# Decoder block on one core: transposed scores in the scores' four PSUM banks, a ring of four banks, and the projection moved ahead of the transposed scores

## What is computed

```python
x = layernorm(x + self_attention(x))        # causal; q and k normed per head, gains, biases
x = layernorm(x + cross_attention(x, ctx))  # rotary q and k, biases
x = layernorm(x + experts(x))               # 8 experts, top 2, 256 -> 512 -> 256, gelu
# attention: dot = q k^T ; att = softmax(dot) ; out = (att v) Wo + bo
```

## Time and profile before

| | us |
|---|---|
| median of 3 runs (lowest, highest) | 1186.8 (1186.4, 1188.1) |
| the profiled execution | 1184.3 |
| its span, first to last instruction | 1182.6 |
| busy in the span: PE / DVE / ACT / POOL | 1033.5 / 720.5 / 597.2 / 268.0 |
| mean granted clock of TensorE, share of full speed | 0.952 |

### The profile page before, as it was taken

One profiled execution on the slowest core, in us unless ns is written; L12 is line 12 of the kernel. 1 busy time (PEld: TensorE's weight loads), 2 busy tenths in 40 slices (PEclk: granted clock), 3 DMA queues, 4 the chain that ended last, 5 costly groups with the idle time before them and its releaser, 6 DMA issues.

```text
span 1182.6 us, 29067 instructions
## 1 busy us (share of the span) xinstructions
PE 1033.5 (87%) x10925; PEld 769.5 (65%) x10925; DVE 720.5 (61%) x1584; ACT 597.2 (51%) x1024; POOL 268.0 (23%) x309
## 2 busy tenths in 40 slices
PE   6899999999999999998999999876379999999930
PEld 3556666666666666666666666544269999999930
DVE  4656666666677777676768777763524444444446
ACT  3567767767755666565555555644122222222225
POOL 1053332322233200001212111132512222222210
PEclk9999999999999999999999999998579999999975
DMA  7117446455440001000000100011167766777656
GB/s 286 29 41 252 136 162 199 133 180 182 132 134 20 20 12 46 11 11 30 30 30 30 36 23 30 12 40 39 68 199 216 215 215 215 216 216 213 204 198 250
DMA packets 95078, 139.25 MB, mean 118 GB/s; under 512 B 11264, under 2 KB 68992, under 8 KB 93920
## 3 DMA queue, kind: packets, MB, share of 16 engines
q1 hardware_dynamic: 88320, 114.98, 31.2%
q0 software_dynamic: 6624, 22.42, 4.9%
HBM read 76.56 MB, written 60.29 MB: 116 GB/s over the span
## 4 chain that ended last, share of the span: by engine, by line
PE 80%; issue 6%; DVE 6%; ACT 4%; DMA 3%; SPq 1%; another core or an unknown queue 0%; ACTq 0%; DVEq 0%; POOLq 0%
PE PS L824 11%; PE PS L561 11%; PE PS L835 10%; PE PS L582 10%; PE PS L531 5%; PE PS L639 5%; PE PS L635 5%; PE PS L706 4%; PE PS L653 4%; PE PS L680 3%; PE PS L538 2%; PE PS L669 2%; ACT pT L904 2%; PE PS L534 2%; DVE part L1158 1%
## 5 line engine op out<-in xcount | busy, mean ns | idle before, releaser
L1158 DVE TENSOR_REDUCE part<-PS 128x6 f32<-128x768 f32 (+1 forms) x256 | 269.9, 1087 | 126.9 <-PE PS L538 84.8
L904 ACT ACTIVATE pT<-PS 128x768 f32<-128x768 f32 (+1 forms) x256 | 220.9, 915 | 94.1 <-PE PS L561 92.1
L561 PE MATMUL PS<-big 32*128 32x256 f32 (+1 forms) x2048 | 133.5, 373 | 21.3 <-issue 13.7
L1595 POOL TENSOR_SCALAR_AFFINE_SELECT pT<-pT 128x512 f32<-128x512 f32 x128 | 84.5, 661 | 279.0 <-ACT pT L904 275.4
L824 PEld LDWEIGHTS PS<-oT,big 128*128 128x128 f32 x1136 | 139.5, 194 | 5.4 <-ACT oT L1034 1.8
L824 PE MATMUL PS<-oT,big 128*128 128x128 f32 x1136 | 140.2, 277 | 1.0 <-ACT oT L1034 1.0
L561 PEld LDWEIGHTS PS<-big 32*128 32x128 f32 x2048 | 96.2, 185 | 64.3 <-issue 62.9
L582 PE MATMUL PS<-pT,vaug 128*32 128x256 f32 (+1 forms) x2048 | 126.3, 364 | 10.4 <-DVE carry L1365 2.3
L835 PE MATMUL PS<-w2s,qkn 128*128 x568 | 134.5, 380 | 0.2 <-issue 0.2
L1034 ACT ACTIVATE oT<-PS 128x256 f32<-128x256 f32 x71 | 27.3, 384 | 191.9 <-PE PS L813 191.9
L915 ACT ACTIVATE oT<-PS 128x256 f32<-128x256 f32 x128 | 49.1, 384 | 143.9 <-PE PS L582 125.0
(11 more groups left out here) (170 smaller groups left out, 1535.9 us busy)
## 6 DMA issues: line engine op xcount, KB each, us to landing
big<-w SPq DMA_DIRECT2D x71, 512.0 KB
xs_dram<-zrow SPq DMA_DIRECT2D x24, 1496.0 KB, 9.2
oT<-xs_dram SPq DMA_DIRECT2D x71, 136.0 KB
xin<-xT SPq DMA_DIRECT2D x16, 256.0 KB, 2.9
w2s<-w POOLq DMA_DIRECT2D x1, 4096.0 KB, 16.4
xb<-x SPq DMA_DIRECT2D x16, 256.0 KB, 11.2
xin<-ctxT SPq DMA_DIRECT2D x16, 256.0 KB, 2.8
big<-nmaxT SPq DMA_DIRECT2D x128, 4.0 KB
```

The source lines that it names most:

```text
L561: ins = pe.matmul(o, keys, a[r0:r1, 0, g, q0:T], start=True, stop=True)
L904: act.activation(pT[:, k % 2, 2 * half:2 * half + 2, 0:wide], src, ACT.Exp).then_inc((exp_a, exp_b)[half], 1)
L1158: dve.tensor_reduce(dst, src, AX.X, ALU.max, negate=True).then_inc((max_a, max_b)[half], 1)
L1595: pool.affine_select(d, d, [[0, 2], [0, 2], [1, P]], ALU.is_ge, 0.0, base=0, channel_multiplier=-1).then_inc(masked, 1)
```

## The change

It gives the transposed scores the same four banks as the scores, and the ring the other four (4 to 7). The score now waits for `exp_b` too, and `score_T` for `max_b` too. On PE `weigh` is followed by the quarter's projection, and `score_T` comes behind it, ahead of the quarter's last turn; for q >= 136, when no scores are left, `score_T` still comes first. `rate` moves ahead of `project_qk` 1, with its place in the ring. ACT's order follows (drains of the projections ahead of `weights`, `exp_gap` at the end); DVE takes the logits in quarter r = 1 instead of r = 2 and both maxima in one go for r = 2; POOL's scatter waits for the next quarter's scores; two start-up results change banks, and one of them is drained a quarter earlier.

```diff
@@ -37,6 +37,8 @@
 NORM_GROUPS = (4, 4, 8, 8, 4, 4)
+
+RING_BANKS = 4
 CHUNKS = 11
@@ -103,10 +105,10 @@
         elif r == 1:
+            n = block_at(q, LOGITS_AT)
+            place("logits", n, n is not None and crossed(n))
             place("qk1", block_at(q, QK_AT + 1))
             place("qT", block_at(q, TURN_Q))
-            n = block_at(q, LOGITS_AT)
-            place("logits", n, n is not None and crossed(n))
         elif r == 2:
@@ -265,8 +267,8 @@
-        S_BANK, ST_BANK = (2, 3, 0, 1), (2, 3, 4, 5)
-        S_HALF, ST_HALF = (PS[:, 1024:2048], PS[:, 0:1024]), (PS[:, 1024:2048], PS[:, 2048:3072])
+        S_BANK = ST_BANK = (2, 3, 0, 1)
+        S_HALF = ST_HALF = (PS[:, 1024:2048], PS[:, 0:1024])
@@ -278,8 +280,7 @@
         xin_in, xb_in = sems("xin_in", 2), sems("xb_in", 2)
-        ring_filled = [sem("ring_filled_0"), sem("ring_filled_1")]
-        ring_drained = [sem("ring_drained_0"), sem("ring_drained_1")]
+        ring_filled, ring_drained = sems("ring_filled", RING_BANKS), sems("ring_drained", RING_BANKS)
         squared, head_var = sem("squared"), sem("head_var")
@@ -329,26 +330,26 @@
         def ring_slot(job):
-            return bank(6 + RING[job] % 2)
+            return bank(RING_BANKS + RING[job] % RING_BANKS)
         def filled_by(job):
-            return ring_filled[RING[job] % 2]
+            return ring_filled[RING[job] % RING_BANKS]
         def drained_by(job):
-            return ring_drained[RING[job] % 2]
+            return ring_drained[RING[job] % RING_BANKS]
...
-            if RING[job] >= 2:
-                pe.wait_ge(drained_by(job), RING[job] // 2)
+            if RING[job] >= RING_BANKS:
+                pe.wait_ge(drained_by(job), RING[job] // RING_BANKS)
...
-            eng.wait_ge(filled_by(job), RING[job] // 2 + 1)
+            eng.wait_ge(filled_by(job), RING[job] // RING_BANKS + 1)
...
-            eng.wait_ge(drained_by(job), RING[job] // 2 + 1)
+            eng.wait_ge(drained_by(job), RING[job] // RING_BANKS + 1)
@@ -509,11 +510,13 @@
                     pe.wait_ge(exp_a, before + 1)
+                    pe.wait_ge(exp_b, before + 1)
                 a = qkT[:, n % 3]
...
                         pe.wait_ge(mask_ready, 1)
+                        pe.wait_ge(bo_ready, 1)
                     for j in range(STRIPS):
@@ -548,6 +551,7 @@
                     pe.wait_ge(max_a, NG * other[0] + other[1] + 1)
+                    pe.wait_ge(max_b, NG * other[0] + other[1] + 1)
                 if k >= 1:
@@ -751,14 +755,14 @@
                 for c in range(KC):
-                    ins = pe.matmul(bank(4)[:, 0:E], bvT[:, c, :], wx_o[:, c, :], start=(c == 0),
+                    ins = pe.matmul(bank(0)[:, 0:E], bvT[:, c, :], wx_o[:, c, :], start=(c == 0),
                                     stop=(c == KC - 1))
...
             for j in range(STRIPS):
-                ins = pe.transpose(bank(5)[:, j * P:(j + 1) * P], columns4[:, j, :], ident[:])
+                ins = pe.transpose(bank(3)[:, j * P:(j + 1) * P], columns4[:, j, :], ident[:])
             ins.then_inc(mask_pe, 1)
@@ -771,24 +775,27 @@
                     score_T(group_at(q, EXP_AT), q)
-                    weigh(group_at(q, WEIGH_AT))
-                else:
-                    weigh(group_at(q, WEIGH_AT))
-                    score_T(group_at(q, EXP_AT), q)
+                weigh(group_at(q, WEIGH_AT))
                 if r == 0:
                     project_qk(block_at(q, QK_AT), 0)
-                    turn_x2(block_at(q, LN_AT))
                 elif r == 1:
+                    rate(block_at(q, LOGITS_AT))
                     project_qk(block_at(q, QK_AT + 1), 1)
-                    turn_qk("qT", block_at(q, TURN_Q), 0)
-                    rate(block_at(q, LOGITS_AT))
                 elif r == 2:
...
                     project_v(block_at(q, V_AT))
-                    turn_qk("kT", block_at(q, TURN_K), 1)
                 else:
...
                     project_o(block_at(q, PROJECT_AT))
+                if q < NG * BLOCKS + SCORE_AT:
+                    score_T(group_at(q, EXP_AT), q)
+                if r == 0:
+                    turn_x2(block_at(q, LN_AT))
+                elif r == 1:
+                    turn_qk("qT", block_at(q, TURN_Q), 0)
+                elif r == 2:
+                    turn_qk("kT", block_at(q, TURN_K), 1)
+                else:
                     count_tokens(routed_at(q, RANK_AT))
@@ -1008,22 +1015,26 @@
                     seed_roots(block_at(q, CHAIN_AT), block_at(q, ROOT_AT))
-                    exp_gap(routed_at(q, RANK_AT))
                     drain_onT(block_at(q, PROJECT_AT))
                 drain_pv(group_at(q, WEIGH_AT))
+                if r == 0:
+                    drain_qk(block_at(q, QK_AT), 0)
+                elif r == 1:
+                    drain_qk(block_at(q, QK_AT + 1), 1)
+                elif r == 2:
+                    drain_v(block_at(q, V_AT))
+                else:
+                    drain_x1T(block_at(q, TURN_X1))
                 weights(group_at(q, EXP_AT), 0)
...
                 if r == 0:
-                    drain_qk(block_at(q, QK_AT), 0)
                     drain_x2T(block_at(q, LN_AT))
                 elif r == 1:
-                    drain_qk(block_at(q, QK_AT + 1), 1)
                     drain_turned("qT", block_at(q, TURN_Q), 0)
                 elif r == 2:
-                    drain_v(block_at(q, V_AT))
                     drain_turned("kT", block_at(q, TURN_K), 1)
                 else:
-                    drain_x1T(block_at(q, TURN_X1))
+                    exp_gap(routed_at(q, RANK_AT))
@@ -1088,7 +1099,7 @@
             dve.wait_ge(mask_pe, 1)
-            dve.tensor_copy(strips[:].rearrange("p j q -> p (j q)"), bank(5)).then_inc(mask_ready, 1)
+            dve.tensor_copy(strips[:].rearrange("p j q -> p (j q)"), bank(3)).then_inc(mask_ready, 1)
             dve.memset(ohb[:], 0.0)
@@ -1135,7 +1146,7 @@
                 dve.wait_ge(vbias_pe, 1)
-                dve.tensor_tensor(bo[:, 1], bank(4)[:, 0:E], bo[:, 1], ALU.add).then_inc(bo_ready, 1)
+                dve.tensor_tensor(bo[:, 1], bank(0)[:, 0:E], bo[:, 1], ALU.add).then_inc(bo_ready, 1)
@@ -1394,12 +1405,12 @@
                     choose_second(routed_at(q, SECOND_AT))
+                    take_logits(block_at(q, LOGITS_AT))
                     rotate(block_at(q, QK_AT + 1), 1)
                 elif r == 2:
-                    take_logits(block_at(q, LOGITS_AT + 1))
                     maxima(group_at(q, SCORE_AT), 0)
+                    maxima(group_at(q, SCORE_AT), 1)
                     divide(block_at(q, OUT_AT), 0)
-                    maxima(group_at(q, SCORE_AT), 1)
                     divide(block_at(q, OUT_AT), 1)
@@ -1418,7 +1429,7 @@
                     take_bias()
-                elif q == 8:
+                elif q == 7:
                     add_folded()
@@ -1607,7 +1618,7 @@
                     ends = nt * TOPK if q == QUARTERS - 1 else min(2 * j + 2, nt * TOPK)
-                    u = group_at(q, SCORE_AT)
+                    u = group_at(q + 1, SCORE_AT)
                     if u is not None:
```

## The result

The changed kernel takes 1363.3 us (median of 3 runs, 1360.9 to 1373.3), against 1186.8: a ratio of 1.150, 95% interval 1.142 to 1.157, 176.5 us more. 1366 had been forecast, in a range of 1338 to 1410.

The account below looks back on a forecast made before the run. PE was taken to bound attention, busy 676.26 of 720 us. Terms 100.2 + 109.3 + 3 - 43.7 + 3 + 8 = 179.8 us, on 1184.3 profiled, gave 1364, as a median 1366 us; range 1338 to 1410.

Parts of the forecast that it names:

- (a): In attention, each next score waits for both halves of the exponentials: 100.2 us in self attention, 109.3 in cross attention.
- (b): Transposed scores wait for both halves' maxima, hidden by PE's work except in five quarters of the last blocks: 3 us.
- (c): In attention, the ring of four and the new order remove all of PE's present idle time: 43.7 us less.
- (d): Delays in ACT's stream before L915, 17.0 us in total, may show in the path: 0 to 17, taken as 3.
- (e): Small edits to DVE's, ACT's and POOL's order and to start-up steps: costed at nothing.
- (f): TensorE's clock falls after half of 18 quarters with 2.25 us idle: 13 us, less 5 for today's falls, +8.
- The rival on the other side: Exponentials finish in time, scores wait for nothing, and up to 43.7 us go: 1143 us; 3 in 100.
- That the clock would swing in every quarter: Each of 122 attention quarters brings one clock fall at 1.4 us, 171 us in all: 1529 us; 7 in 100.

Follow-up runs that it names:

- e2: Kernel before, own banks and ring of two kept, with the projection moved ahead of the transposed scores and its drain ahead of the exponentials: 1291.0 us, ratio 1.096.
- e4: Changed kernel with the exponential of half b taken twice, one after the other: 1613.0 us, ratio 1.355 to the kernel before.
- e7: Kernel before with only the router's matmuls, their ring place and DVE's drain moved as in the change: 1167.6 us, ratio 0.981; on another chip (e7b) 1155.7, 0.983.
- e3: Changed kernel with a ring of two banks and DVE's first division between the two maxima again: 1380.1 us, ratio 1.172 to the kernel before.
- e1: Changed kernel with the projection back behind the transposed scores, shared banks and ring of four kept: 1308.4 us, ratio 1.110 to the kernel before.
- e6: Changed kernel with turn x1T moved behind the transposed scores in each cross block's fourth quarter: 1337.6 us, ratio 1.135 to the kernel before.

## Why the prediction was right

The mechanism was right. That the number came out within 0.2% was luck in part: the clock cost 13 us more than forecast, and PE's idle time came 25 us under its forecast, some 8 of which are only counted as busy instead. The errors cancel. What the span of the profiled execution grew by, with the stretch from 60 us to the last score taken for attention:

| | forecast, us | measured, us |
|---|---|---|
| idle time before the scores | 209.5 | 189.3 |
| PE's other idle time in attention: removed waits, maxima, ACT | -43.7 + 3 + 3 | -42.6 |
| falls of the clock, attention and behind | 8 | 20.9 |
| PE's busy time otherwise, attention | 0 | 7.8 |
| behind the last score, without the clock | 0 | 1.2 |
| sum | 179.8 | 176.6 |

(a) **The loop** was the mechanism, and its price was read right. From the transposed scores to the next score 2.69 us were worked out and 2.65 measured in self attention (the last latency is 0.14, not 0.19), 3.33 and 3.30 in cross attention; over all 122 quarters that is 362.6 us against 365.3. e2 and e4 show it from either side: an exponential less on the loop, and one more. The waits sum to 191.6 us (189.3 behind 60 us), not 209.5, in part because a row's idle time counts from the modelled end of the last matmul (0.94 us after its start), while I took distances between starts (0.86); what is not counted as idle there is counted as busy, most of the 8 us in the table. A self block in mid-kernel grew by 5.4 us (21.8 to 27.2); the forecast's terms make 6.3, less the 0.6 that PE idled in it before. The small rest isn't resolved further.

(b) **The maxima** were covered, as said: between 60 and 907 us no transposed scores wait. At the end of attention five do, 0.27 to 0.75 us each, 2.7 in all, where 3 were forecast.

(c) **The removed waits** went nearly altogether: between 60 us and the last score PE now idles 192.0 us, 189.3 of them before the scores, so that 2.7 are left of 45.3. e7 shows that 2% of gain was there without the loop, e3 that the ring of four saves 26 us in the new order, some of it time that a ring of two would add, and not time that the kernel before lost.

(d) **ACT's unnamed waits**, 17.0 us before the change, don't appear before L922, its line in the changed kernel. 3 us were charged, none came: the 2.7 us of idle time left in attention are those of (b).

(e) The edits costed at nothing: nothing in the rows contradicts it in mid-kernel; there the loop keeps its 2.65 and 3.30 us in every quarter. The 5.9 us added behind the last score were not in the sum. In this stretch PE was busy at a clock of 0.50 for 27.9 us, against 18.2 before, which accounts for 4.8 of them. It need not be the change: e7 and e7b, one kernel, took 396.4 and 389.7 us here.

(f) **The clock** was the undersized term: +8 forecast, some 21 measured. Between 60 us and the last score it fell 12 times and PE was busy at 0.50 for 45.9 us, against 4 times and 13.7 us before. Half of the difference, 16.1 us, is what that costs; the price of one fall was right (1.57 us, 9.19 less 7.62, against 1.4). The other 4.8 us lie behind the last score, as said. Of the 18 quarters with the long gap I had counted half and then taken off 5 us for today's falls. Of the 19 gaps of 1.9 us or more 13 were followed by a fall. The Trainium skill says that small idle times between groups of matmuls can make the clock swing ("TensorE: Matmul & The Clock Gate", "A second HAM failure mode: psum-queue depth-cycling"). e4's trace agrees. The changed kernel's self-attention blocks don't, with a gap of 1.1 or 1.7 us in each quarter and not one fall from 60 to 504 us, while e3, with the same gaps, had five falls up to 440 us.

The rival on the other side asked whether the loop binds at all: e1, e2 and e4 answer it. That the clock would swing in every quarter did not come true; e4, with an exponential more, came nearer to it with 79 falls.

## What to carry to other kernels

Two products that share a buffer form a loop through every engine that empties it; before sharing, add up the loop (here score, maxima, transposed scores, exponentials) and compare it with the work that the order leaves to cover each part. One projection can cover either the maxima or the exponentials, not both. With own banks for one half the kernel before waited 13.7 us for the maxima with the projection on the exponentials; with the projection on the maxima even these banks didn't save it (e2, 9.6%). Of a change in many pieces try each alone: the small move of the router's matmuls gave 2%, inside a change that cost 15%. And a sum that agrees to 0.2% is to be taken apart before it is believed: here a clock term that was 13 us short was hidden by idle time that had been forecast too long.

## What the runs showed of the hardware that was not expected

The share of PE's gaps that a fall of the clock follows rises steeply with their length. Counted from 60 us on by the score's wait for ACT, by the trace's record of the granted clock, and as followed where a fall starts between 1.0 us before and 2.6 us after the start of that score:

| | wait, us | followed by a fall |
|---|---|---|
| changed kernel, to 900 us | 1.1 to 1.7 | 0 of 98 |
| changed kernel, to 900 us | 1.9 and 2.1 | 9 of 14 |
| e3 | 1.7 | 6 of 32 |
| e4 | 2.0 | 16 of 31 |
| e4 | 2.4 and 2.6 | 45 of 69 |
| e4 | 3.0 to 3.2 | 17 of 19 |

Length alone doesn't decide. In the changed kernel the eight router blocks had their fall in the same quarter, and these falls start 34.1 us apart (599.7, 633.9, 668.0 and so on to 838.7) while a block takes 33.9 us. The first starts 0.1 us after the start of the score, the eighth 1.6 us after it; behind the next such score, at 871.10 with a wait of 1.94, there is none, and four gaps of the same 2.15 us between 511 and 568 us had none either. So where in time the gap falls counts too, and eight falls in a row belong to the rhythm of this kernel; the shares above hold for these rhythms, and what they would be in another isn't shown. No run moved a gap in time at the same length.

Where a gap can't be avoided, a piece of work moved into it can pay more than its own length: e6 moved one turn in each cross block; the quarter that it left got 0.4 us shorter and a router block 1.8.
